# Context loaded already turned; its layer norm's deviations applied at the scores' maximum and at the copy of the turned probabilities

## The reference, cut to what matters

```python
x1 = layernorm(_layernorm(x), ln1_g, ln1_b);  x2 = layernorm(ctx, ln2_g, ln2_b)
q, k, v = x1 @ Wq + bq, x2 @ Wk + bk, x2 @ Wv + bv
attn = softmax(einsum('bqe,bke->bqk', q, k) * E ** -0.5)
x = x + einsum('bqk,bke->bqe', attn, v) @ Wo + bo
# experts: n = _layernorm(x); top 3 of 31 gates of softmax(n @ Wr + br)
x = x + gelu(n @ ws1 + bs1) @ ws2 + bs2 + sum(gate_e * (gelu(n @ We1[e] + Be1[e]) @ We2[e] + Be2[e])) + n
```

## Time and profile before

| | us |
|---|---|
| median of 3 runs | 479.38 (479.09 to 480.47) |
| the profiled execution | 478.4 |
| its span, first to last instruction | 476.7 |
| TensorE busy | 453.9 (95%) |
| VectorE busy | 374.1 (78%) |
| ScalarE busy | 261.6 (55%) |
| GpSimd busy | 240.2 (50%) |

### The profile page before, as it was taken

One profiled execution on the slowest core, in us unless ns is written; L12 is line 12 of the kernel. 1 busy time (PEld: TensorE's weight loads), 2 busy tenths in 40 slices (PEclk: granted clock), 3 DMA queues, 4 the chain that ended last, 5 costly groups with the idle time before them and its releaser, 6 DMA issues.

```text
span 476.7 us, 13393 instructions
## 1 busy us (share of the span) xinstructions
PE 453.9 (95%) x3168; PEld 400.5 (84%) x3168; DVE 374.1 (78%) x1622; ACT 261.6 (55%) x873; POOL 240.2 (50%) x322
## 2 busy tenths in 40 slices
PE   8899999999999999889999999999999999999993
PEld 8687877777777777678999999999999999999993
DVE  4979999999999997784777777777767777772897
ACT  1556757676767766563666665555555555553220
POOL 4222667758585857671456556444444444443000
PEclk9999999999999999989999999999999999999997
DMA  8574666768554614673566666544444444433996
GB/s 240 133 230 155 200 219 208 231 211 253 156 185 139 187 37 167 222 282 94 151 193 199 193 192 200 158 141 139 137 141 136 141 137 138 137 115 116 406 399 226
DMA packets 53452, 87.51 MB, mean 184 GB/s; under 512 B 7969, under 2 KB 31650, under 8 KB 53378
## 3 DMA queue, kind: packets, MB, share of 16 engines
q1 hardware_dynamic: 43170, 60.69, 42.6%
q0 software_dynamic: 9168, 25.49, 14.1%
q10 hardware_dynamic: 1040, 0.48, 0.6%
HBM read 55.02 MB, written 31.61 MB: 182 GB/s over the span
## 4 chain that ended last, share of the span: by engine, by line
PE 60%; DVE 23%; POOL 4%; issue 4%; DMA 3%; ACT 1%; SPq 0%; DVEq 0%; POOLq 0%; ACTq 0%
PE bank L1281 20%; PE bank L1292 19%; DVE base L1037 5%; PE bank L1270 5%; DVE w_all L794 3%; POOL expert_rows_in L552 2%; DVE w1b_all L746 2%; PE bank L1117 2%; PE bank L1116 2%; PE bank L1168 2%; PE bank L1128 2%; PE bank L1169 1%; DVE base L1030 1%; DMA w_all<-routed_rows 1%; DVE negmax L768 1%
## 5 line engine op out<-in xcount | busy, mean ns | idle before, releaser
L567 POOL DMA_INDIRECT routed_rows<-tok,token x105 | 101.5, 967 | 107.6 <-DVE tok L986 95.6
L685 ACT ACTIVATE up<-bank,b_all 128x128 f32<-128x128 f32 x260 | 81.1, 363 | 97.7 <-PE bank L1281 64.2
L1281 PE MATMUL bank<-tok,w1b_all 128*128 128x128 f32 x840 | 111.0, 275 | 0.0
L1292 PE MATMUL bank<-w_all,up 128*128 x420 | 108.1, 380 | 0.0
L1281 PEld LDWEIGHTS bank<-tok,w1b_all 128*128 128x128 f32 x840 | 102.1, 192 | 0.1
L986 DVE TENSOR_SCALAR tok<-bank,gate,inverse 128x256 f32<-128x256 f32 x105 | 57.0, 543 | 51.1 <-PE bank L1292 50.8
L552 POOL DMA_INDIRECT expert_rows_in<-xt,slot x75 | 74.2, 989 | 21.2 <-issue 20.6
L1292 PEld LDWEIGHTS bank<-w_all,up 128*128 128x128 f32 x420 | 71.8, 191 | 5.4
L716 ACT ACTIVATE tok<-bank 128x256 f32<-128x256 f32 x105 | 40.2, 383 | 32.4 <-PE bank L1270 31.8
L978 DVE COPY w1b_all<-w_all 128x512 f32 x105 | 44.9, 428 | 3.8 <-issue 1.7
L1270 PE MATMUL bank<-ident,xt 128*128 128x128 f32 x210 | 40.1, 273 | 0.5 <-DMA xt<-expert_rows_in 0.5
(11 more groups left out here) (206 smaller groups left out, 904.6 us busy)
## 6 DMA issues: line engine op xcount, KB each, us to landing
xt<-expert_rows_in SPq DMA_DIRECT2D x105, 133.0 KB
w_all<-in_w SPq DMA_DIRECT2D x44, 256.0 KB, 4.6
w_all<-in_ctx SPq DMA_DIRECT2D x32, 288.0 KB, 3.3
w_all<-routed_rows SPq DMA_DIRECT2D x5, 1152.0 KB, 13.3
base<-in_x SPq DMA_DIRECT2D x25, 128.0 KB, 3.4
w_all<-routed_rows SPq DMA_DIRECT2D x4, 768.0 KB, 14.5
expert_rows_in<-pad_rows SPq DMA_DIRECT2D x21, 133.0 KB, 2.6
w_all<-in_w SPq DMA_DIRECT2D x2, 1280.0 KB
```

Of the source, the lines that this page charges most:

```text
L567: pool.indirect_dma_start(routed_rows, bass.IndirectOffsetOnAxis(ap=token[sx][:, 0:1], axis=0), y_sb[sx], None).then_inc(put[sx], 16)
L685: ins = act.activation(up[s][:, m * P:m * P + P], up_ps[s][:, m * P:m * P + P], ACT.Gelu, bias=b1_all[:, e, m:m + 1].rearrange("p o n -> p ...
L1281: mm = pe.matmul(up_ps[s][:, m * P:m * P + P], w[:, c * INTER + m * P:c * INTER + m * P + P], xtt[s][:, c * P:c * P + P], start=(c == 0), ...
L1292: mm = pe.matmul(down_ps[s], up[s][:, m * P:m * P + P], w, start=(m == 0), stop=(m == 1))
```

## The change

- The context comes twice from memory: as before, but raw into six buffers `c_sb` of 193 columns (`CS`), with keys dealt in threes (partition p holds keys 3p to 3p+2), and turned, (192, 361), into `ct0` and `ct1`. The normalised copy `z`, its normalisation, its six transposes and the two copies from PSUM are gone.
- A mean's share is folded into the weights (`part_0`, `part_1`, `wsum`, products with `g2_s`), so that raw context can stand where c - mean stood. In the last column of `c_sb` and the last row of `ct1` stands 1/rstd in the place of the ones: (variance + eps) * rstd, which GpSimd makes with two multiplications.
- rstd along the keys is needed as a row. SyncE stores both numbers of each key to device memory (`store_devs`), waits until they have landed, and loads them back (`load_devs`): one row into `ct1`, the other spread over 100 partitions (`dev_row`).
- VectorE multiplies the scores by `dev_row`, writes them to `probs` and takes the maximum in the same instruction; the negation is an instruction of its own. ScalarE takes the exponential in place.
- The turned probabilities are multiplied by rstd, a scalar of each partition then, in the copy from PSUM, now three copies.

```diff
 def load_ctx(b):
-    if b >= SLOTS:
-        sp.wait_ge(ctx_norm, b + 1 - SLOTS)
+    if b >= CS:
+        sp.wait_ge(mix_made, b + 1 - CS)
...
+def store_devs(b):
+    sp.wait_ge(ctx_dev, b + 1)
+    alone(sp)
+    sp.dma_start(dev_rows[b].rearrange("n (p k) -> p n k", k=3),
+                 st(b - 2)[:, 0:3, 2:4].rearrange("p k n -> p n k")).then_inc(rows_out[b % 4], 16)
+
+def load_turned(b):
+    if b >= 2:
+        sp.wait_ge(scores_made, b - 1)
+        alone(sp)
+    sp.dma_start(ct0[b % 2], ctx_t[b, 0:P, :]).then_inc(ct_in[b % 2], 16)
+    sp.dma_start(ct1[b % 2][0:D2B, :], ctx_t[b, P:D2, :]).then_inc(ct_in[b % 2], 16)
+
+def load_devs(b):
+    sp.wait_ge(rows_out[b % 4], (b // 4 + 1) * 16)
+    if b >= 2:
+        sp.wait_ge(rowmax_made, b - 1)
+    alone(sp)
+    sp.dma_start(ct1[b % 2][D2B:D2C, :], dev_rows[b, 0:1, 0:LK]).then_inc(ct_in[b % 2], 16)
+    sp.dma_start(dev_row[b % 2], dev_rows[b, 1, 0:LK].partition_broadcast(LQ)).then_inc(row_in[b % 2], 16)
...
 def step(i):                                  # SyncE
+    if batch(i + 1) is not None:
+        store_devs(i + 1)
+        load_turned(i + 1)
     if batch(i + 4) is not None:
         load_ctx(i + 4)
     if starts(i + 4) is not None:
         load_x(starts(i + 4))
+    if batch(i + 1) is not None:
+        load_devs(i + 1)
...                                            # then the loads of w1 and w2, as before
-    if i == B - 1:
-        sp.wait_ge(ctx_norm, B)
+    if i == B:
+        sp.wait_ge(scores_made, B)
+        sp.wait_ge(rowmax_made, B)
         late2(18, 22)
-    if i == B + 1:
-        sp.wait_ge(scores_made, B)
+    if i == B + 2:
         sp.wait_ge(x_transposed, TILES)
+        sp.wait_ge(mix_made, B)
         late2(22, 26)
...                                            # GpSimd, behind L526
+if b is not None:
+    pool.wait_ge(ctx_rstd, b + 1)
+    pool.tensor_tensor(c_sb[b % CS][:, :, D2], m[:, 0:3, 2], m[:, 0:3, 3], ALU.mult).then_inc(ctx_last, 1)
+    pool.wait_ge(ctx_last, b + 1)
+    pool.tensor_tensor(m[:, 0:3, 2], m[:, 0:3, 2], m[:, 0:3, 3], ALU.mult).then_inc(ctx_dev, 1)
...                                            # ScalarE
-act.activation(zt0[s], zt_ps0[:, 0:LK], ACT.Copy)
-act.activation(probs_t[s][:, 0:2, :], probs_ps[:, 0:2 * LQ].rearrange("p (t q) -> p t q", q=LQ), ACT.Copy)
-act.activation(probs_t[s][0:KT[2], 2, :], probs_ps[0:KT[2], 2 * LQ:3 * LQ], ACT.Copy).then_inc(probs_t_copied, 1)
-act.activation(zt1[b % 2], zt_ps1[0:D2C, 0:LK], ACT.Copy).then_inc(ctx_t_copied, 1)
+for k in range(3):
+    ins = act.activation(probs_t[s][0:KT[k], k, :], probs_ps[0:KT[k], k * LQ:(k + 1) * LQ], ACT.Copy,
+                         scale=st(b - 2)[0:KT[k], k, 3:4])
-act.activation(probs[s], bank[s][0:LQ, 0:LK], ACT.Exp, bias=negmax[s][:, 0:1]).then_inc(probs_made, 1)
+act.wait_ge(negmax_made, b + 1)
+act.activation(probs[s], probs[s], ACT.Exp, bias=negmax[s][:, 0:1]).then_inc(probs_made, 1)
...                                            # VectorE
-dve.tensor_reduce(negmax[s][:, :], bank[s][0:LQ, 0:LK], AX.X, ALU.max, negate=True).then_inc(rowmax_made, 1)
+dve.wait_ge(row_in[s], (rated // 2 + 1) * 16)
+dve.tensor_tensor_reduce(probs[s], bank[s][0:LQ, 0:LK], dev_row[s], 1.0, LOWEST, ALU.mult, ALU.max,
+                         rowmax[s][:, :]).then_inc(rowmax_made, 1)
...                                            # behind the router logits, L774
+dve.tensor_scalar(negmax[s][:, :], rowmax[s][:, :], -1.0, None, ALU.mult).then_inc(negmax_made, 1)
-for k in range(3):
-    ins = dve.tensor_scalar(z[s4][:, k, 0:D2], c_sb[s4][:, k, :], st(i - 1)[:, k, 0:1],
-                            st(i - 1)[:, k, 3:4], ALU.subtract, ALU.mult)
...                                            # setup; for wk_aug and again for wv_aug
+for c in range(2):
+    dve.tensor_tensor_reduce(bank[3][:, c * D2:c * D2 + D2], wk_aug[:, c, 0:D2], g2_s, 1.0, 0.0, ALU.mult, ALU.add,
+                             wsum[:, c:c + 1]).then_inc(scaled, 1)
+for c in range(2):
+    dve.tensor_scalar(wk_aug[:, c, 0:D2], bank[3][:, c * D2:c * D2 + D2], -float(D2), wsum[:, c:c + 1], ALU.mult,
+                      ALU.add).then_inc(aug_ready, 1)
...                                            # TensorE
-for k in range(3):
-    pe.transpose(zt_ps0[:, k * P:k * P + n], z[s4][0:n, k, 0:P], ident[0:n, 0:n])
-    mm = pe.transpose(zt_ps1[0:D2C, k * P:k * P + n], z[s4][0:n, k, P:D2 + 1], ident[0:n, 0:n])
-mm = pe.transpose(probs_ps[0:n, k * LQ:(k + 1) * LQ], probs[s][:, k * P:k * P + n], ident[0:LQ, 0:LQ])
+mm = pe.transpose(probs_ps[0:n, k * LQ:(k + 1) * LQ], probs[s][:, k:LK:3], ident[0:LQ, 0:LQ])
```

More of the change, by code:

```diff
@@ L28 @@
 SCALE = float(E) ** -0.5
+LOWEST = -3.0e38
 D2B = D2 - P
 D2C = D2B + 1
-KT = [P, P, LK - 2 * P]
+KT = [len(range(k, LK, 3)) for k in range(3)]
 TOKENS = B * LQ
@@ L54 @@
 XS = 6
+CS = 6
 SPARE = XS * P
@@ L488, in _ @@
             const(pool.memset(eps_cols[:, 4:5], EPS))
-            for s in range(SLOTS):
-                const(pool.memset(z[s][:, :, D2:D2 + 1], 1.0))
             const(pool.affine_select(out=tri[:, :], in_=tri[:, :], compare_op=ALU.is_gt, fill=0.0,
@@ L578, in _ @@
             act.dma_start(cols_s[:, :], cols).then_inc(cols_in, 16)
-            act.dma_start(rows_s.rearrange("p c n -> p (c n)"), rows.partition_broadcast(P)).then_inc(cols_in, 16)
+            act.dma_start(rows_s, rows.partition_broadcast(P)).then_inc(cols_in, 16)
             act.dma_start(wr_s[:, :, :], wr.rearrange("(c p) e -> p c e", p=P)).then_inc(router_in, 16)
@@ L596, in step @@
             def step(i):
-                b = batch(i)
-                if b is not None:
-                    s = b % 2
-                    act.wait_ge(ctx_transposed, b + 1)
-                    if b >= 2:
-                        act.wait_ge(scores_made, b - 1)
-                    act.activation(zt0[s], zt_ps0[:, 0:LK], ACT.Copy)
                 b = batch(i - 2)
@@ L609, in step @@
                         act.wait_ge(mix_made, b - 1)
-                    act.activation(probs_t[s][:, 0:2, :], probs_ps[:, 0:2 * LQ].rearrange("p (t q) -> p t q", q=LQ), ACT.Copy)
-                    act.activation(probs_t[s][0:KT[2], 2, :], probs_ps[0:KT[2], 2 * LQ:3 * LQ],
-                                   ACT.Copy).then_inc(probs_t_copied, 1)
-                b = batch(i)
-                if b is not None:
-                    act.activation(zt1[b % 2], zt_ps1[0:D2C, 0:LK], ACT.Copy).then_inc(ctx_t_copied, 1)
+                    act.wait_ge(ctx_rstd, b + 1)
+                    for k in range(3):
+                        ins = act.activation(probs_t[s][0:KT[k], k, :], probs_ps[0:KT[k], k * LQ:(k + 1) * LQ], ACT.Copy,
+                                             scale=st(b - 2)[0:KT[k], k, 3:4])
+                    ins.then_inc(probs_t_copied, 1)
                 t = starts(i)
@@ L739, in step @@
             def step(i):
-                new, met, rated = batch(i + 2), batch(i + 1), batch(i - 1)
+                new, rated = batch(i + 2), batch(i - 1)
                 new_x, met_x = starts(i + 2), starts(i + 1)
@@ L775, in step @@
                                              ALU.add).then_inc(logit_sum, 1)
+                if rated is not None:
+                    dve.wait_ge(rowmax_made, rated + 1)
+                    dve.tensor_scalar(negmax[s][:, :], rowmax[s][:, :], -1.0, None, ALU.mult).then_inc(negmax_made, 1)
                 if routed is not None:
@@ L898, in _ @@
                 dve.tensor_tensor_reduce(bank[2][:, c * D2:c * D2 + D2], wv_aug[:, c, 0:D2], b2_row, 1.0, bv_s[:, c:c + 1], ALU.mult, ALU.add,
-                                         wv_aug[:, c, D2:D2 + 1]).then_inc(aug_ready, 1)
+                                         wv_aug[:, c, D2:D2 + 1])
+            dve.wait_ge(aug_ready, 2)
+            for c in range(2):
+                dve.tensor_tensor_reduce(bank[3][:, c * D2:c * D2 + D2], wv_aug[:, c, 0:D2], g2_s, 1.0, 0.0, ALU.mult, ALU.add,
+                                         wsum[:, 2 + c:3 + c]).then_inc(scaled, 1)
+            dve.wait_ge(scaled, 4)
+            for c in range(2):
+                dve.tensor_scalar(wv_aug[:, c, 0:D2], bank[3][:, c * D2:c * D2 + D2], -float(D2), wsum[:, 2 + c:3 + c], ALU.mult,
+                                  ALU.add).then_inc(aug_ready, 1)
             step(-1)
-            dve.tensor_scalar(qs0[:, 0:1], g2_0, SCALE, None, ALU.mult).then_inc(dve_chain, 1)
-            dve.wait_ge(dve_chain, 9)
-            dve.tensor_scalar(qs1[0:D2C, 0:1], g2_1, SCALE, None, ALU.mult).then_inc(dve_chain, 1)
-            dve.wait_ge(dve_chain, 10)
+            dve.tensor_scalar(qs0[:, 0:1], part_0, SCALE, None, ALU.mult).then_inc(dve_chain, 1)
+            dve.wait_ge(dve_chain, 11)
+            dve.tensor_scalar(qs1[0:D2C, 0:1], part_1, SCALE, None, ALU.mult).then_inc(dve_chain, 1)
+            dve.wait_ge(dve_chain, 12)
             dve.wait_ge(folds_made, 2)
@@ L1088, in _ @@
             turn_x(0)
-            turn_ctx(0)
             pe.wait_ge(fold_q_ready, 1)
```

(5 more changed lines are left out.)

115 lines of the change are left out of this document (52 added, 63 removed).

## The result

The changed kernel takes 539.53 us in the median of 4 runs (535.5 to 540.92), the kernel before, run beside it on the same chip, 479.93 (479.09 to 480.8): a ratio of 1.123, 95% interval 1.120 to 1.126. The profiled span grew from 476.7 to 536.8 us.

What follows compares the result with a forecast made beforehand. TensorE and VectorE looked nearly full in the first stage, GpSimd worked without pause in scatter steps. From 478.4 us profiled: start +1.0, maxima 0 to 19 +3.1, 19 to 29 -2.3, rest 0: 480.2, median 481, range 469 to 492.

Steps and rivals of the forecast that it cites:

- L: Landing time of SyncE's store of the deviations, taken as 3.6 us; a SyncE step is at least this plus 2.0.
- small stores have nothing to move: Argument for the rival that GpSimd alone decides: SyncE's store lands in 3.2 us or less; chance 0.27.
- The page weighed against it: Skill page's DMA figures for SyncE's store: landing estimated at 2.1 us, SyncE step 4.1; used in none of the sums.
- have little left, and landings get longer: DMA engines in steps that load weights: 5.8 us of work in a step of 5.6, so landings lengthen.
- GpSimd 5.91 us in a scatter step: GpSimd's two added multiplications, 0.58 us, lengthen its steps with scatters from 5.33 to 5.91 us.
- The rival that GpSimd alone decides: First stage: L is 3.2 or less, SyncE's step 5.2, GpSimd sets the pace; 475.6 us, chance 0.27.
- VectorE and TensorE get room: First stage: VectorE loses 0.98 us a step and gets 0.3; TensorE loses 0.62 a batch; both get idle time.
- Steps 19 to 29 go by GpSimd at 5.44: Maxima 19 to 29, w2 no longer loaded: GpSimd sets 5.44 us a step, 54.4 against 56.7, -2.3 us.
- Start +1.0 (0 to 3): Setup before the first scores: VectorE's added products and the first store's round trip delay them by 1.0 us.
- End 0: Last steps and all after: last weights issued some 7 us later, covered before the second stage; no cost.
- The round trip costs more: SyncE's wait for `rows_out` decides from L = 3.6 up: 491.6 us at 4.2, 499 at 4.6; chance 0.28.

## Why the prediction was wrong, by its own steps

- **The failed step: "For L ... take 3.6."** It measured 6.1 in the median (3.9 in the first step, issued at 14.46 and read at 18.35). The form was right: landing plus four issues, the turned and context loads hidden inside. With 6.1, and 1.6 instead of 2.0 for the issues, the prediction's own sum gives 19 x 7.7 = 146.3 against 104.3, +42, for the first 19 steps. The first 19 steps took 145.3 by the maxima. It took L from transfers of large pieces and a count of the bytes ahead in the queue; the earlier trace rows has 3.43 us a MB with pieces of some 1.7 KB (12.75 MB in 7552). The same view of the changed kernel:

```profile
q1 hardware_dynamic: 14132, 13.55, 75.4%
```

  13.55 MB in 60.3 of 80 us is 4.45 us a MB, with nearly twice the packets. The store's 256 pieces weren't priced at all (a rival even had it that "small stores have nothing to move"), nor were the finer cut of the context and 100 reads of one row. The runs bound the parts: with the store and the wait but none of the change's loads, L is 4.8; with them 6.1; with them and half the pieces of the store 5.0.
- **The page weighed against it.** The Trainium skill, "DMA: Bandwidth & Descriptors", section "Anatomy of one DMA", made L 2.1 by my estimate. The trace disagrees: 3.8 in the shortest landing, 6.1 in the median. The section's 2 us are a fit for DMAs that GpSimd issues, which the prediction didn't say; the store is SyncE's. Two other places of the same page of the Trainium skill fit better and I hadn't used them: "Specifications" wants 512 bytes or more a transfer, below which the engines read, modify and write (12 bytes here; halving their number gave 25.6 us), and "Latency and other measured facts" has memory's own latency ten times longer under load. The runs show the price of pieces, not its mechanism; neither sentence was tested.
- **DMA engines "have little left, and landings get longer".** Right in direction. It was counted as 5.8 us of a step of 5.6 and then not used in L beyond the bytes ahead.
- **GpSimd 5.91 us in a scatter step.** Mis-sized: 6.20 in the kernel before with the two multiplications added, 6.13 to 6.31 in the run without a trip. 0.87 instead of 0.58: the starts are 0.27 apart, near the 0.29 that I took (80.83, 81.10), but the first scatter behind them comes later by more than that. (The reading of the earlier trace rows was too neat as well: of its 7 waits four are long, in steps without scatters, and three are of about 0.5 us in steps with them.) In the changed kernel this is covered by SyncE, which is why its 12 us show only when the trip is gone. The rival that GpSimd alone decides (475.6) would have been about 487, as that run shows.
- **VectorE and TensorE get room.** Right, and worth about 5 us (474.7 against 480) beside GpSimd's old work, never seen in the change.
- **Steps 19 to 29 go by GpSimd at 5.44.** Wrong: 7.10, since the landing decides there too. Even in the last steps, with two turned loads behind it and no weights, SyncE's timeline has the store issued at 235.49 and 240.79 and its reader at 240.13 and 245.13, 4.6 and 4.3 us; the 3.6 was never reached.
- **Start +1.0 (0 to 3).** It was 2.6. The first store was issued at 14.46, as forecast (14.6), and landed 3.9 us later instead of 2.6. **End 0.** 60.1 in the span less 55.3 and 2.6 leaves 2.2 for the last two steps and what follows.
- **"The round trip costs more", 0.28.** This rival named place and mechanism, but its end, 499 at 4.6, took the slowest landing of a trace whose queues had none of the new pieces in them.

As differences of runs, in this order: wait 34, small store 15, repeated read 4.5, GpSimd's multiplications 12, and 5 gained: 539.5 to 505.9, 491.4, 486.9, 474.7. Another order would share them otherwise: half the store's pieces alone gave 25.6 while the wait was in place, since a shorter landing makes the wait shorter.

## What to carry to other kernels

A wait for a transfer's landing in the queue that also issues the next loads makes each step at least that landing plus the issues behind it. Size the landing with the change's own traffic in the queue, and by its pieces as well as its bytes. A 3 KB store in 12-byte pieces was free where everything was loaded four steps ahead, and cost tens of microseconds where one load had to come back in the step. When a busy engine is relieved, look first at the one that seems idle but works without a pause (GpSimd here): 0.4 us of new work there gave away twice what the change gained.

## What the runs showed of the hardware

- A 3 KB store to device memory in 256 pieces a step raised the DMA share from 0.70 to 0.98 and the median landing of a 288 KB load from 3.0 to 6.5 us, at the same time of the kernel.
- Its own packets take 9 ns each; others took up to twice as long in the mean (1024 bytes: 53 to 108 ns) at the same median. Half the pieces of twice the size, waited for in each step, made its landing 5.0 instead of 6.1 us.
- 100 reads of one row of device memory cost 4.5 to 5.6 us over 32 batches against 100 rows. Behind 100 reads of one SBUF partition, the issue of the second weight took 3.3 to 3.9 us.
- Two dependent 0.2 us instructions on GpSimd lengthened its step by 0.87 us.
- An f32 transpose on TensorE is one instruction, an f32 product of the same columns two: 0.32 against 0.61 us.
